# Relational graph convolution with residual LayerNorm on one core: a fourth tile of the second half from TensorE in every other turn, and a reordered first turn

## The reference

```python
h = feat[src]
def step(m, rw):
    r, w_r = rw
    mask = jnp.where(etypes == r, 1.0, 0.0).astype(h.dtype)
    return m + mask[:, None] * (h @ w_r), None
m, _ = jax.lax.scan(step, m0, (jnp.arange(n_rels), weight))
out = jax.ops.segment_sum(m, dst, num_segments=feat.shape[0])
x = _layernorm(x + out, axis=-1)
```

## Time and profile before

| | us |
|---|---|
| median of 3 runs (793.82 to 796.39) | 793.93 |
| the profiled execution, its own time | 793.14 |
| its span, first to last instruction | 791.3 |
| POOL busy in the span, 603 instructions | 564.9 (71%) |
| PE busy | 673.4 (85%) |
| DVE busy | 639.9 (81%) |
| ACT busy | 621.7 (79%) |
| mean granted TensorE clock | 0.971 |

### The profile page before, as it was taken

How to read it: one execution, slowest core, us unless ns; L and a number is a source line. 1 busy time by engine, 2 the same in 40 slices (tenths; PEclk the granted TensorE clock), 3 DMA queues, 4 the chain that set the end, 5 groups by cost and what they waited for, 6 DMA issues and landing times.

```text
span 791.3 us, 24924 instructions
## 1 busy us (share of the span) xinstructions
PE 673.4 (85%) x8446; PEld 648.6 (82%) x8447; DVE 639.9 (81%) x2221; ACT 621.7 (79%) x1232; POOL 564.9 (71%) x603
## 2 busy tenths in 40 slices
PE   0679999889888889888989989899898889888856
PEld 0579999889888889888889889899888889888845
DVE  5988988788787788787788887789787789788914
ACT  5589988788888788787888878788788788888613
POOL 2747777777777777777777777777777777777760
PEclk9999999999999999999999999999999999999975
DMA  9222232222222222223222222222222222322111
GB/s 210 76 54 67 75 76 76 68 72 76 75 65 76 72 68 76 71 69 76 72 67 76 76 66 75 74 65 76 72 70 74 74 64 76 76 66 61 49 51 42
DMA packets 30424, 57.81 MB, mean 73 GB/s; under 512 B 11864, under 2 KB 16082, under 8 KB 30410
## 3 DMA queue, kind: packets, MB, share of 16 engines
q0 software_dynamic: 18848, 38.64, 19.0%
q1 hardware_dynamic: 11254, 18.19, 8.4%
q10 hardware_dynamic: 308, 0.80, 0.5%
HBM read 55.19 MB, written 2.40 MB: 73 GB/s over the span
## 4 chain that ended last, share of the span: by engine, by line
POOL 46%; issue 22%; DMA 10%; PE 9%; ACT 6%; DVE 6%; POOLq 0%; ACTq 0%; DVEq 0%
POOL rows L306 46%; DMA rows<-x_parts,gidx 9%; PE own L728 5%; ACT aggT L369 4%; DVE pick L505 3%; PE agg L760 3%; DMA x_sb<-in_x 1%; ACT pick L395 1%; PE rel L773 1%; PE own L867 1%; PE own L799 0%; DVE x_sb L644 0%; POOLq L199 0%; DVE src_f L558 0%; DVE tmin L531 0%
## 5 line engine op out<-in xcount | busy, mean ns | idle before, releaser
L306 POOL DMA_INDIRECT rows<-x_parts,gidx x589 | 559.2, 949 | 200.8 <-issue 177.3
L505 DVE TENSOR_SCALAR pick<-src_h,node 125x516 bf16<-125x516 f16 (+1 forms) x1240 | 445.2, 438 | 103.6 <-ACT src_h L357 103.6
L728 PE MATMUL own<-xp,pick 125*128 125x192 bf16 x5425 | 472.1, 249 | 18.4 <-issue 10.2
L728 PEld LDWEIGHTS own<-xp,pick 125*128 125x128 bf16 x5425 | 454.1, 99 | 31.6 <-issue 16.9
L760 PE MATMUL agg<-onehot,rows 128*128 128x112 bf16 x2418 | 140.4, 215 | 68.2 <-DMA rows<-x_parts,gidx 68.2
L389 ACT ACTIVATE away<-src_h,node_neg 125x516 bf16<-125x516 f16 (+1 forms) x310 | 186.9, 666 | 6.9
L760 PEld LDWEIGHTS agg<-onehot,rows 128*128 128x128 bf16 x2418 | 125.8, 99 | 78.6 <-issue 76.3
L395 ACT ACTIVATE pick<-away,one 125x516 bf16<-125x516 bf16 (+1 forms) x310 | 186.7, 672 | 0.0
L571 DVE TENSOR_SCALAR onehot<-ramp,krel 128x112 bf16<-128x112 bf16 x806 | 148.9, 261 | 0.0
L369 ACT ACTIVATE aggT<-agg 64x512 f32<-64x512 f32 x124 | 73.3, 591 | 73.0 <-PE agg L760 71.5
L403 ACT ACTIVATE rows<-own 128x384 bf16<-128x384 f32 x93 | 45.6, 490 | 58.1 <-PE own L728 54.2
(11 more groups left out here) (67 smaller groups left out, 98.8 us busy)
## 6 DMA issues: line engine op xcount, KB each, us to landing
rows<-x_parts,gidx POOLq DMA_INDIRECT x589
src_b<-in_src SPq DMA_DIRECT2D x31, 258.0 KB
src_b<-in_src SPq DMA_DIRECT2D x31, 192.0 KB
x_parts<-xp SPq DMA_DIRECT2D x1, 728.0 KB
x_parts<-xp SPq DMA_DIRECT2D x1, 672.0 KB
out<-x_sb SPq DMA_DIRECT2D x2, 224.0 KB
x_sb<-in_x ACTq DMA_DIRECT2D x1, 364.0 KB
x_sb<-in_x ACTq DMA_DIRECT2D x1, 336.0 KB
```

The lines of the kernel that those rows point to most:

```text
L306: pool.indirect_dma_start(rows[:, u, j, :], None, x_parts, bass.IndirectOffsetOnAxis(ap=gidx[:, u, j:j + 1], axis=0)).then_inc(rows_in[u] ...
L505: v.tensor_scalar(pick[u][:, b, :], src_h[u][:, :, 0:CUTW[u]], node[:, b:b + 1], None, ALU.is_equal).then_inc(pick_ready[u], 1)
L728: return nc.tensor.matmul(own_slot(u, h), pick[u][:, b, h * P:(h + 1) * P], xp[:, b, 0:SPLIT, :].rearrange("p s d -> p (s d)"), start=(b = ...
```

## The change

PE fetches four tiles of the second half in the odd turns and three in the even ones. `OWN` becomes (4, 4) and stands for the widest case; `FEWER = 3` is the count in even turns. The loop now holds two turns, an odd and an even one, and runs 14 times for the turns 1 to 28; turn 29 is written out as well. In an even turn POOL gathers the fourth tile of the second half first, on a semaphore of its own, `fourth_in`, for which PE waits ahead of that tile. In an odd turn that gather is gone. With turns 0, 2, ... 30 at 19 gathers and turns 1, 3, ... 29 at 18 there are 574 instead of 589. SP spreads 516 sources instead of 384 for the second half in every turn.

The order changes in three places. Ahead of the loop DVE makes the first picks before it works out windows and keys, PE makes its first products before it transposes the keys, and ACT follows that order. In turn 0 PE aggregates both halves before the products of turn 1. And on ACT `group_indices` stands earlier: for half 0 ahead of the last picks of that half, for half 1 ahead of `take_agg(i, 1)`.

```diff
-    OWN = (4, 3)
+    OWN = (4, 4)
+    FEWER = 3
...
+            with eng.Fori(0, LAST // 2 - 1) as k:
+                body(k * 2 + 1, True)
+                body(k * 2 + 2, False)
+            body(LAST - 1, True)
...
+        def own_count(u, odd):
+            return OWN[u] if u == 0 or odd else FEWER
+        def cut_width(u, odd):
+            return CUTW[u] if own_count(u, odd) == OWN[u] else FEWER * P // CUT
...
+                if own_count(u, odd) == FEWER:
+                    pool.indirect_dma_start(
+                        rows[:, u, FEWER, :], None, x_parts,
+                        bass.IndirectOffsetOnAxis(ap=gidx[:, u, FEWER:FEWER + 1], axis=0)).then_inc(fourth_in, 16)
                 for j in range(OWN[u], GT):
...
+            dve.wait_ge(const_set, 5)
+            picks(0, 0, False)
             step(v.tensor_reduce(tmin[:, :], tile_view(dst_f), AX.X, ALU.min))
...
-            picks(0, 0)
+            picks(0, 1, False)
             dve.wait_ge(krel_done, 2)
...
             onehots(0, 0)
-            picks(0, 1)
+            onehots(0, 1)
...
                 if more:
-                    act_picks(i + 1, 0, 3)
+                    group_indices(i + 1, 0)
+                    act_picks(i + 1, 0, 3, not odd)
                 take_agg(i, 0)
...
+                    act_picks(i + 1, 1, 3, not odd)
+                    group_indices(i + 1, 1)
                 take_agg(i, 1)
...
+                    if j == FEWER and own_count(u, odd) == FEWER:
+                        pe.wait_ge(fourth_in, (i // 2 + 1) * 16 if isinstance(i, int) else (i + 2) * 8)
...
+            def turn(i, odd, more=True):
+                fetch_own(i, 1, odd)
+                if is_first(i):
+                    pe.wait_ge(par_in, 16)
+                    aggregate(i, 0, odd, window_starts(i, 0))
+                    aggregate(i, 1, odd, window_starts(i, 1))
+                    fetch_own(i + 1, 0, not odd)
+                    pe.wait_ge(w_centered, 2)
+                    return
```

More of the change, by code:

```diff
@@ L259, in _, with turn @@
                     sp.dma_start(pv[p0:p1, b0:b1, :], xp[p0:p1, b0:b1, :, :].rearrange("p b s d -> p b (s d)")).then_inc(parts_out, 16)
-            def turn(i):
+            def turn(i, odd):
                 spread_sources(i, 0)
@@ L298, in _, with fetch @@
             pool.wait_ge(parts_out, 64)
-            def fetch(i, u):
+            def fetch(i, u, odd):
                 if not is_first(i):
@@ L308, in fetch, with turn @@
                         bass.IndirectOffsetOnAxis(ap=gidx[:, u, j:j + 1], axis=0)).then_inc(rows_in[u] if j < LATE else late_in[u], 16)
-            def turn(i):
-                fetch(i, 0)
-                fetch(i, 1)
+            def turn(i, odd):
+                fetch(i, 0, odd)
+                fetch(i, 1, odd)
             group_loop(pool, turn)
@@ L388, in act_picks @@
                     for b in range(b0, b1):
[L389 removed]
+                        last = act.activation(away[:, b, 0:CUT * cut_width(u, odd)].rearrange("p (c w) -> p c w", c=CUT), src_h[u][:, :, 0:cut_width(u, odd)], ACT.Abs,
                                               bias=node_neg[:, VPICK + b:VPICK + b + 1])
@@ L394, in act_picks, with take_pair @@
                     for b in range(b0, b1):
-                        last = act.activation(pick[u][:, VPICK + b, :], away[:, b, 0:OWNW[u]], ACT.Relu, bias=one[:, :], scale=-1.0)
+                        last = act.activation(pick[u][:, VPICK + b, 0:CUT * cut_width(u, odd)], away[:, b, 0:CUT * cut_width(u, odd)], ACT.Relu, bias=one[:, :], scale=-1.0)
                     if part == 3:
                         last.then_inc(act_pick_ready[u], 1)
-            def take_pair(i, u, k):
-                act.wait_ge(own_done[u], i * OWN[u] + (2 * k + 2))
+            def take_pair(i, u, k, odd):
+                act.wait_ge(own_done[u], i * 2 + (k + 1))
                 pair = own_pair(2 * u + k)
[L403 to L410, removed]
+                n = min(2, own_count(u, odd) - 2 * k)
+                act.activation(rows[:, u, 2 * k:2 * k + n, 0:SPLIT * D], pair[:, 0:n, 0:SPLIT * D], ACT.Copy).then_inc(own_rows[u], 1)
+                act.activation(rows[:, u, 2 * k:2 * k + n, SPLIT * D:RP * D], pair[:, 0:n, 0:D], ACT.Copy).then_inc(own_rows[u], 1)
             def take_rel(i):
@@ L419, in _ @@
             group_indices(0, 0)
+            narrow_sources(0, 0, False)
+            act.wait_ge(const_set, 5)
+            act_picks(0, 0, 0, False)
+            act_picks(0, 0, 1, False)
             group_indices(0, 1)
+            act_picks(0, 0, 2, False)
+            act_picks(0, 0, 3, False)
             act.wait_ge(et_in, 64)
             act.activation(et_f[:, :], et_i[:, :], ACT.Copy).then_inc(et_cast, 1)
[L423 to L426, removed]
+            narrow_sources(0, 1, False)
+            act_picks(0, 1, 0, False)
+            act_picks(0, 1, 1, False)
+            act.wait_ge(zeros_set, 1)
+            clear_agg(0)
+            take_pair(0, 0, 0, False)
+            take_pair(0, 0, 1, False)
+            act_picks(0, 1, 2, False)
+            act_picks(0, 1, 3, False)
             act.wait_ge(krelT_done, 1)
@@ L616, in _, with turn @@
             dve.wait_ge(out_zeroed, 1)
-            def turn(i, more=True):
+            def turn(i, odd, more=True):
                 if more:
-                    picks(i + 1, 0)
+                    picks(i + 1, 0, not odd)
                 else:
@@ L628, in turn @@
                 if more:
-                    picks(i + 1, 1)
+                    picks(i + 1, 1, not odd)
                     onehots(i + 1, 0)
@@ L636, in _ @@
                             AX.X, ALU.max).then_inc(any_set, 1)
-            turn(LAST, more=False)
+            turn(LAST, False, more=False)
             def finish(n):
@@ L729, in product @@
                                             xp[:, b, 0:SPLIT, :].rearrange("p s d -> p (s d)"), start=(b == 0), stop=(b == NB - 1))
-                for h in range(OWN[u]):
+                for h in range(own_count(u, odd)):
                     if u == 1 and h == 2:
@@ L738, in fetch_own @@
                         last = product(h, b)
-                    last.then_inc(own_done[u], 1)
+                    if h == 1 or h == own_count(u, odd) - 1:
+                        last.then_inc(own_done[u], 1)
             def window_starts(i, u):
```

99 lines of the change are left out of this document (40 added, 59 removed).

## The result

The changed kernel takes 777.12 us (median of 4 runs, 776.47 to 778.50) against 795.16 us in the runs of the same session: ratio 0.9772, 95% interval 0.9751 to 0.9794. Five more runs in a later session gave 776.13 against 795.28, ratio 0.9757 (0.9740 to 0.9775). The forecast was 776.3 us and a ratio of 0.978.

A forecast was written before the change was run, and what follows sets the result against it. POOL's gathers were taken to bound the kernel: 17.5 us from fewer gathers plus 0.1 from the start gave 17.6, so 793.14 to 775.5 profiled; adding 0.79 for the median gave 776.3 us, range 774 to 779.

The forecast's parts named there:

- POOL bounds, 1.248 us a gather, 17.5 us from turn 2 on: From turn 2's first gather POOL never waits, so 14 gathers less at 1.248 us each save 17.5 us.
- The number: Forecast median of the changed kernel: 776.3 us, own range 774 to 779, chance 0.66; span 773.7 us.
- The pair of turns: Compute engines need 23.3 us for an odd turn, 21.6 for an even, 44.9 together, against POOL's 46.2: margin 1.3.
- POOL's idle time moves one half on: Most of POOL's 8.46 us wait behind turn 0 moves to turn 1's second half, starting at 66.0 against 67.36.
- The clock: PE, idle 4.0 us before turn 1's products, runs at 1.2 GHz: loss 1.55 us, ends 0 and twice that.
- The loop of two turns: The longer loop isn't loaded anew each pass: 0 us; rival, loaded anew each pass: 832 us, chance 0.04.
- DVE's longer picks and POOL: Rival: DVE's picks, 1.4 us longer in each odd turn, hold POOL up, costing 21 us: 797 us, chance 0.02.
- The wait for rows in every pair: Sign of being right: PE still waits for gathered rows in every pair of turns, but shorter; no size given.

## Why the prediction was right

- **POOL bounds, 1.248 us a gather, 17.5 us from turn 2 on.** Right. Leaving out the gathers without any work in their place gives the same pace, and the alternation alone gives the whole gain.
- **The number.** The median, 777.12 us, is 0.8 above the forecast, and part of that nearness is luck: the span, 775.7, is 2.0 above its forecast of 773.7. The start was 1.6 us later than forecast and the pace cost 1.3, of which the long gather and the tail gave back 0.9. The median then lay 0.4 below the profiled execution (777.51), where I had added 0.79.
- **The pair of turns.** I had 44.9 us for the compute engines, measured are 45.4, so the margin is 0.8 us and not 1.3. The even turn (21.59) was right. The odd one took 23.79, where I had 23.3: I let PE's next products start right behind the aggregation, but the transposition (0.27 us) and a pause of 0.35 us stand between, which the wait for DVE's picks had covered in the earlier trace rows. The margin was smaller than thought, but held; with four tiles in every turn it is gone.
- **POOL's idle time moves one half on.** Right: 66.0 forecast, 67.40 measured. The 1.4 us between are the clock: with PE kept busy it is 65.68.
- **The clock.** I took one loss of 1.55 us and named two as the end. It was two, 1.5 and 1.65 us: turn 2's gathers start at 81.38, not at 79.7. This is the mis-sized term, 1.6 us too small. The idle time of 4.0 us that I had in view came as 0.94 and 2.33, with the second aggregation between them. The second idle time, 2.77 us ahead of the other 100 products, I hadn't seen: the aggregation that stood between the two groups has moved ahead of both, and PE waits in its place for ACT's picks. With PE kept busy the start is 78.01, and I had 78.2 for it.
- **The loop of two turns.** Nothing, as forecast: one packet in 580 us, and no slower pace in the kernel that has the loop and 589 gathers.
- **DVE's longer picks and POOL.** No effect on the gathers' length. My sign for it, gathers longer than 944 ns, came up in the profile after (947), but the same kernel's later trace has 945, as has the one without the long picks in odd turns, and the kernel with long picks in every turn has 944.
- **The wait for rows in every pair.** Wrong in its place: up to about 430 us PE comes later than the rows, since it began 81 us in and gains only 0.8 us a pair; from there on it waits again, once a pair and for 0.2 to 0.5 us, where before it was some 2 us and 0.7 us a turn. That it would be shorter was right.
- What I didn't give enough weight is the reordering. By itself it is worth 2 to 3 us; with four tiles in turn 1 nothing is left of them (the last gather starts at 752.82, and at 753.03 without the reordering).

## What to carry to other kernels

Where one engine works without a pause, count its operations: the gain is their number times the pace, and other engines' work is free until their own pace for a whole turn comes up to it. Measure that second pace where stocks are full, and add what a wait covers there (a transposition, an issue pause), since it comes out when the wait goes. If work alternates between heavy and light turns, let the light one come first: the start is where the compute engines are late, and there each microsecond counts in full.

## What the runs showed of the hardware

- The length of an idle time by itself didn't tell what the clock did to the 100 products behind it: 8.42 us behind 2.77 us of idle time in one kernel, 10.01 behind 2.80 in another, 10.08 behind 1.93 in the changed kernel's later trace. In the profile after, the granted clock was 0.50 (1.2 GHz) from 54 to 56 us and 1.00 from 58 on. With 22 and 26 products of zeros in the two gaps it stayed at 1.00, and the five times lay within 0.9 us, against 2.7 us without them.
- A loop of twice the length, 549 matrix products (565 rows of the trace) and what lies between them on PE, had one packet on the instruction queues in 580 us. The Trainium skill (Runtime: NRT & Kernel Launch, "Instruction fetch mechanics") gives PE room for 2048 instructions, with which this agrees.
- On one chip the kernel before took 1.7 times as long (1368 us), and kernels like the changed one 1360 to 1365 us, with PE's products 0.7 to 2.1 us apart in the stretch shown, and gathers at 0.94 us. Where the chips differ isn't to be seen in the traces.
